# First norm's factor applied to token-major rows on VectorE and the rows transposed on TensorE, with new orders on every engine

## The reference

```python
h = _ln(x, ln1_g, ln1_b)                      # 16 heads of 16, rotary embedding, causal
a = _attn(rope(h @ sa_wq + sa_bq) * scale, rope(h @ sa_wk + sa_bk), h @ sa_wv + sa_bv)
x = x + (a @ sa_wo + sa_bo)
h = _ln(x, ln2_g, ln2_b)                      # queries from h, keys and values from the context y
a = _attn(rope(h @ ca_wq + ca_bq) * scale, rope(y @ ca_wk + ca_bk), y @ ca_wv + ca_bv)
x = x + (a @ ca_wo + ca_bo)
h = _ln(x, ln3_g, ln3_b)
x = x + (gelu(h @ fc1_w + fc1_b) @ fc2_w + fc2_b)
attn = softmax(ctx @ x.T); ti = attn @ x      # scores of the context against the result
out = tanh(cat([ctx, ti]) @ trans_W + trans_b) + ctx
```

## Time and profile before

| what | value |
|---|---|
| median of 3 runs | 3593.34 us (3587.76 to 3603.11) |
| profiled execution | 3593.57 us, its span 3591.8 us |
| granted TensorE clock, mean | 0.907 of 2.4 GHz |
| busy: PE, PEld, DVE, ACT, POOL | 84%, 72%, 63%, 63%, 27% of the span |
| moved by DMA | 173.42 MB, mean 48 GB/s |

### The profile page before, as it was taken

How to read it: one execution, slowest core, us unless ns; L and a number is a source line. 1 busy time by engine, 2 the same in 40 slices (tenths; PEclk the granted TensorE clock), 3 DMA queues, 4 the chain that set the end, 5 groups by cost and what they waited for, 6 DMA issues and landing times.

```text
span 3591.8 us, 92602 instructions
## 1 busy us (share of the span) xinstructions
PE 3031.7 (84%) x38640; PEld 2587.0 (72%) x38640; DVE 2256.0 (63%) x5290; ACT 2271.7 (63%) x4874; POOL 960.5 (27%) x1164
## 2 busy tenths in 40 slices
PE   3578888888888888888888888888888888888897
PEld 3457777777777777777777777777777777777786
DVE  3466666666666666666666666666666666666673
ACT  1246666666666666666666666666666666666676
POOL 1222222222222222222222222222222223223221
PEclk6778989989999999999999999999899899899899
DMA  3111111111111121111111211111111211111110
GB/s 93 36 42 43 47 54 45 47 54 45 47 53 45 47 55 46 50 51 45 50 51 47 53 46 47 53 47 45 53 45 47 53 45 46 53 46 47 52 32 27
DMA packets 299731, 173.42 MB, mean 48 GB/s; under 512 B 68100, under 2 KB 297476, under 8 KB 299044
## 3 DMA queue, kind: packets, MB, share of 16 engines
q1 hardware_dynamic: 298448, 164.36, 16.9%
q10 hardware_dynamic: 864, 3.15, 0.2%
HBM read 81.31 MB, written 16.84 MB: 27 GB/s over the span
## 4 chain that ended last, share of the span: by engine, by line
DMA 39%; PE 25%; DVE 17%; SPq 7%; issue 4%; ACT 4%; POOL 3%; another core or an unknown queue 0%; DVEq 0%; POOLq 0%
DMA rstd_rows<-rstd 22%; DMA rb<-rstd_rows 12%; DVE z_s L740 6%; DMA qkt_s<-rp_s 4%; SPq L242 4%; SPq L249 3%; DVE z_c L740 3%; PE B L384 3%; PE A L610 2%; PE A L384 2%; PE B L386 2%; PE B L385 2%; PE C L384 2%; PE C L385 2%; PE C L386 2%
## 5 line engine op out<-in xcount | busy, mean ns | idle before, releaser
L1061 ACT ACTIVATE pt<-sc 128x512 f32<-128x512 f32 x1024 | 528.9, 603 | 122.2 <-PE sc L413 88.3
L1239 POOL TENSOR_TENSOR rstd<-var_eps,mhalf 128x1 f32<-128x1 f32 x384 | 269.3, 701 | 834.2 <-DVE var_eps L659 834.2
L1234 POOL TENSOR_TENSOR rp_s<-tq_s,cst 128x512 f32<-128x512 f32 x128 | 166.7, 1302 | 837.3 <-ACT tq_s L1053 837.3
L898 DVE TENSOR_TENSOR rows_in<-rows_in,rb 128x256 f32<-128x256 f32 x128 | 57.4, 449 | 420.0 <-DMA rb<-rstd_rows 419.9
L740 DVE TENSOR_REDUCE z_c<-sc 128x8 f32<-128x1024 f32 x256 | 300.7, 1217 | 24.1 <-PE sc L413 24.0
L740 DVE TENSOR_REDUCE z_s<-sc 128x8 f32<-128x1024 f32 x256 | 300.9, 1218 | 0.6 <-PE sc L403 0.6
L1041 ACT CAST qk_bf_s<-qkt_s 128x1024 bf16<-128x1024 f32 x128 | 135.2, 1056 | 245.8 <-DMA qkt_s<-rp_s 245.8
L1041 ACT CAST qk_bf_c<-qkt_c 128x1024 bf16<-128x1024 f32 x128 | 134.8, 1053 | 227.0 <-DMA qkt_c<-rp_c 227.0
L1234 POOL TENSOR_TENSOR rp_c<-tq_c,cst 128x512 f32<-128x512 f32 x128 | 163.4, 1276 | 324.8 <-ACT tq_c L1053 324.8
L413 PE MATMUL sc<-qk_bf_s 31*128 31x128 bf16 x2048 | 59.5, 242 | 216.1 <-ACT qk_bf_s L1041 216.0
L413 PEld LDWEIGHTS sc<-qk_bf_s 31*128 31x128 bf16 x2048 | 34.0, 102 | 264.2 <-ACT qk_bf_s L1041 243.6
(11 more groups left out here) (207 smaller groups left out, 11126.7 us busy)
## 6 DMA issues: line engine op xcount, KB each, us to landing
rows_in<-in_ctx_t SPq DMA_DIRECT2D x256, 128.0 KB, 2.8
qkt_s<-rp_s SPq DMA_DIRECT2D x512, 64.0 KB
qkt_c<-rp_c SPq DMA_DIRECT2D x512, 64.0 KB, 3.6
rows_in<-in_x SPq DMA_DIRECT2D x128, 128.0 KB, 2.9
rows_in<-in_x_t SPq DMA_DIRECT2D x128, 128.0 KB, 2.1
out<-o_out SPq DMA_DIRECT2D x128, 128.0 KB, 3.0
rb<-rstd_rows SPq DMA_DIRECT2D x128, 64.0 KB, 4.8
qkt_s<-zt_s SPq DMA_DIRECT2D x512, 2.0 KB
```

Source lines behind the costliest of these rows:

```text
L1061: act.activation(pt[:, r, :, :].rearrange("p g q -> p (g q)"), sc[:, r, :], ACT.Exp).then_inc(signal, 1)
L1234: pool.tensor_tensor(rp[c][:, :].rearrange("p (a q) -> p a q", q=P), tq[c][:, :].rearrange("p (a q) -> p a q", q=P), rope_c[:, :].unsqueez ...
L1239: pool.tensor_tensor(out[:, :], var_eps[k - 1][:, :], mhalf[:, :], ALU.pow).then_inc(s[f"rs{k}"], 1)
```

## The change

- `x_t`, its load, `rstd_rows`, `rb`, `rbw_`, `rbr_` and `xs_` are gone. `xn_` on DVE multiplies the token-major rows `x_in` by the factor of their partition, `trx1_` on TensorE transposes the result into bank `A0`, and `xt_hi_` and `xt_lo_` read from there.
- `xt_hi` and `xt_lo` hold three tiles; `sq_` takes its pair from them as a view of two thirds, in one pair of three with a backward stride.
- The rings change: `x_in` 5 (3), `ct_f` 3 (4), `ct_g` 2 (1), `cw` 9 (11), `xres_c` 4 (3). `ftan_` writes `o_out` and `fout_` adds in place; `fpre` is gone.
- Every engine has a new order, new offsets of its steps, other waits, and other banks for many results: the transposes, `f1a` and `sq` in `A0`, `pv_s`, `y_c`, `vs`, `cvt`, `fy` in `A1`, `cp`, `pv_c`, `y_s`, `f1b`, `fs`, `trfa` in `B0`. There are 144 slots for 142. The work of each step is otherwise the same.

```diff
-        xt_hi, xt_lo = [sb(f"xt_{p}", [P, KC, M * P], F32R) for p in ("hi", "lo")]
+        xt_hi, xt_lo = [sb(f"xt_{p}", [P, KC, 3 * P], F32R) for p in ("hi", "lo")]
...
-            def rbw_(t):
-                if live(t):
-                    sp.wait_ge(s["rs1"], done(t))
-                    sp.dma_start(rstd_rows[t % 4].unsqueeze(1), rstd1[t % 2][:, :]).then_inc(rbw[t % 2], 16)
-            def rbr_(t):
-                if live(t):
-                    sp.wait_ge(rbw[t % 2], 16 * (t // 2 + 1))
-                    sp.dma_start(rb[t % 2][:, :], rstd_rows[t % 4].partition_broadcast(P)).then_inc(rbr[t % 2], 16)
...
-            def xs_(t):
-                if live(t):
-                    dve.wait_ge(ld_t[t % 2], 16 * (t // 2 + 1))
-                    dve.wait_ge(rbr[t % 2], 16 * (t // 2 + 1))
-                    rows = xt_f[t % 2].rearrange("p (k q) -> p k q", k=KC)
-                    dve.tensor_tensor(rows, rows, rb[t % 2][:, :].unsqueeze(1).broadcast_to([P, KC, P]), ALU.mult).then_inc(s["xs"], 1)
+            def xn_(t):
+                if live(t):
+                    dve.wait_ge(s["rs1"], done(t))
+                    dve.tensor_scalar(xn[:, :], x_in[t % 5], rstd[0][:, 0:1], None, ALU.mult).then_inc(s["xn"], 1)
...
+            def trx1_(t):
+                if live(t):
+                    if t <= 4:
+                        pe.wait_ge(s["xn"], done(t))
+                    if t <= 4:
+                        need(pe, s["tq_s"], pairs(t - 1))
+                    need(pe, s["x2t_lo"], done(t - 5))
+                    transposes(A0, xn[:, :], KC).then_inc(s["trx1"], 1)
...
+            def xt_hi_(t):
+                if live(t):
+                    act.wait_ge(s["trx1"], done(t))
+                    copy(third(xt_hi, t), per_k(A0), s["xt_hi"])
...
+            def pair_of(a, t):
+
+                first = (t - 1) // M * M % 3
+                thirds = [a[:, k, :].rearrange("p (j q) -> p j q", j=3) for k in range(KC)]
+                return [v[:, ::-2, :] if first == 2 else v[:, first:first + M, :] for v in thirds]
...
+                    pair_projection(A0, "sqk", 2 * ((t - 1) % M), pair_of(xt_hi, t), pair_of(xt_lo, t)).then_inc(s["sq"], 1)
```

More of the change, by code:

```diff
@@ L158, in build @@
         zd_s, zd_c = [[sem(f"zd_{c}{i}") for i in range(2)] for c in "sc"]
-        names = ("st1", "mv1", "ve1", "rs1", "xs", "xt_hi", "xt_lo", "vs", "v_s", "sq", "tq_s", "cos_s", "rot_s", "add_s",
+        names = ("st1", "mv1", "ve1", "rs1", "xn", "trx1", "xt_hi", "xt_lo", "vs", "v_s", "sq", "tq_s", "cos_s", "rot_s", "add_s",
                  "kr_s", "p1s", "max_s", "zt_s", "p2s", "exp_s", "pv_s", "ot_s", "rinv_s", "att_s", "norm_s",
@@ L448, in f2, with f2a_ @@
                 mm.then_inc(signal, 1)
[L450 to L464, removed]
             def trx2_(t):
                 if live(t):
-                    if t <= 6:
-                        pe.wait_ge(s["x2n"], done(t))
-                    transposes(A1, x2n[:, :], KC).then_inc(s["trx2"], 1)
+                    pe.wait_ge(s["x2n"], done(t))
+                    transposes(A0, x2n[:, :], KC).then_inc(s["trx2"], 1)
+            def f2a_(t):
+                if live_pair(t):
+                    if t >= TILES - 5:
+                        pe.wait_ge(s["hla"], pairs(t))
+                    f2(t, 0, "a", s["f2a"])
             def p2s_(t):
@@ L519, in p2c_, with trx3_, f2b_ @@
                     heads(qkt["c"][:, t % 4, G:2 * G, :], qkt["c"][:, t % 4, 0:G, :], 2 * HD, True).then_inc(s["p2c"], 1)
+            def trx3_(t):
+                if live(t):
+                    if t >= TILES - 4:
+                        pe.wait_ge(s["xh3"], done(t))
+                    need(pe, s["xt_lo"], done(t + 9))
+                    transposes(A0, xhat[:, :], KC).then_inc(s["trx3"], 1)
+            def f2b_(t):
+                if live_pair(t):
+                    if t >= TILES - 6:
+                        pe.wait_ge(s["hlb"], pairs(t))
+                    f2(t, 1, "b", s["f2b"])
             def y_c_(t):
@@ L580, in p1c_, with trf_ @@
                     pe.wait_ge(s["kr_c"], done(t))
[L581 removed]
+                    if t <= 3:
+                        need(pe, s["max_s"], 2 * done(t + 3))
                     heads(qk_bf["c"][:, 0:G, :], qk_bf["c"][:, G:2 * G, :], MX, True).then_inc(s["p1c"], 1)
[L584 removed]
+            def trf_(t):
                 if live(t):
[L586 to L588 removed]
+                    if t >= TILES - 4:
+                        need(pe, s["x3"], pairs(t + 2) // 2)
+                    need(pe, s["tq_s"], pairs(t + 12))
+                    if t >= TILES - 6:
+                        need(pe, s["ghia"], pairs(t + 3))
+                    transposes(A0, x3[t % R][:, :], KC).then_inc(s["trf"], 1)
@@ L1335, in layouts @@
     out["ctx_t"] = by_feature(out.pop("ctx_1024"))
-    out["x_t"] = by_feature(out["x"])
     def halves_first(w):
```

839 lines of the change are left out of this document (410 added, 429 removed).

## The result

The kernel after takes 2827.38 us (median of 3 runs, 2826.17 to 2829.15) where the kernel before takes 3593.34: a ratio of 0.787, 95% interval 0.784 to 0.789. The direction, the mechanism and the new bound are as forecast; the size is not.

What follows compares the result with a forecast made beforehand. It took the latency of the rstd_rows/rb round trip as the bound, TensorE's queue next: 25 set-up + 224 fill + 114 x 22.1 (2519) + 207 end = 2975 us of span, 2977 us in all; range 2885 to 3230.

Steps and rivals of the forecast that it cites:

- `sq`'s 3-D operand: Operand pairs of sq read on TensorE as a 3-D pattern, one in three with backward stride; cost taken as 0.
- Rival A: New order of ACT or DVE becomes the bound; TensorE idles up to 2.3 us a slot: 24.0, 3210 us; chance 22%.
- B: TensorE was already the bound, the transposes add 40 us: 3633 us, slower; 6% together with dearer 3-D operands.
- C: Another transfer, the four of zt_c before the spread, keeps the period at 26.7: about 3600 us; chance 4%.
- period: Steady time per tile, set by TensorE: 21.39 plus 0.31 for transposes plus 0.37 for hand-overs, 22.07, say 22.1 us.
- fill of 14 slots: First 14 part-filled slots of the pipeline, at 16 us each, the middle between 11.6 and 21.4: 224 us.
- drain: End after the last full slot: 185 us of before plus 22 for one more slot, 207 us.
- the 0.37 us a tile for small hand-overs: TensorE's waits for ot_c and xt_lo in the steady part of before, added to the new slot: 0.37 us a tile.
- the gapless slot: Slot in the old kernel's drain after the last round trip, TensorE busy without a gap: 21.39 us, the period's base.
- `trx1` at 0.31 us: Two added transposes of xn on TensorE, priced like trx2's spacing, nothing hidden: 0.31 us a tile.
- floor, 21.6: Slot behind the range's lower end: 21.6 us with a fill of 200, giving 2885 us.
- ACT's room: ACT's work between f1b's end and p2c's start, about 7.6 us against TensorE's 8.4: fits by 0.8 us.

Runs made afterwards that it cites:

- e1: Kernel before, old orders, without the round trip's write and read; rows of ones replace the factor: 2866.3 us, ratio 0.809.
- e11: Kernel after with x2n and xhat on ACT computing only 32 of their 256 columns: 2827.19 us, ratio 0.820 to before.
- e4: Kernel after with the two transposes of xn (trx1) made twice: 2850.33 us, ratio 0.805 to before.
- e8: Kernel after without trx1 and xn; x_t loaded again, factors turned on DVE, sent through DRAM in four pieces: 2822.92 us, ratio 0.817 to before.
- e5: Kernel after with x2n computed twice on ACT in each slot: 2888.66 us.
- e10: Kernel before, old orders, factors turned on DVE and written as four pieces of 128 bytes, read as before: 2950.45 us, ratio 0.854.
- e9: Kernel before with the 128 factors written 64 bytes apart; the read takes an input row instead: 2884.74 us.
- e7: Kernel after with the old round trip put back at the end of SP's slot, xn waiting for it: 4064.99 us.
- e2: Kernel before with both transfers still issued, but DVE doesn't wait for them and multiplies by ones: 3396.9 us.
- e3: Kernel before with the 128 factors written 512 bytes apart; the read takes an input row instead: 2883.63 us.

## Why the prediction was off

What held: the mechanism (the round trip bounded the kernel, TensorE's queue comes next) and its signs, namely no `rstd_rows` and no `rb` in the chain; the chain 94% TensorE; clock 0.99 over the span; no wait of `kr_s` for its spread (it lands in 2.2 us, not the 3.6 taken); nothing lost by `sq`'s 3-D operand: its group takes 1.61 us in every pair of the kernel after, and as much in e1 where it isn't held up. Rival A fell by the period and by e11, B by e1, C by the period.

The profiled execution took 2829.15 us for its span of 2827.4, the same 1.8 outside it that the prediction added. So the miss is taken between the spans, 2975 - 2827 = 148 us, and it goes by terms:

| term | predicted | measured | us in the total |
|---|---|---|---|
| period | 22.1 | 21.093 | 113 x 1.007 = 114 |
| full slots | 114 | 113 | 22 |
| set-up | 25 | 21.1 | 4 |
| fill of 14 slots | 224 | 222.6 | 1 |
| drain | 207 | 200.1 | 7 |

The period is the term that failed, and in three parts of it. First, the 0.37 us a tile for small hand-overs, carried over from the steady part of before: in e1 none of them shows as a wait of the matmuls, and what is left of `xt_lo`'s is within its 21.33. It was within the 21.39 of the drain too (there `xt_lo` ends at 3416.69 and `sq` starts at 3416.74). So the gapless slot was the right base as it stood, and to add hand-overs to it was the mistake. Second, `trx1` at 0.31 us: 0.207 by e4, 0.15 by e8. Third, a part that the prediction put at nothing: the new order itself. The kernel after less `trx1` has 21.093 - 0.207 = 20.89, the old order in e1 21.33, with the same matmuls and a granted clock of 1.00 in both. That is 0.44 us a tile, 50 us in all; by e8, which has no `trx1` and 20.97, it is 0.36. With 0.06 of the base (21.39 for 21.33) and 0.03 of rounding (22.07 to 22.1) the parts make up the 1.007. In a slot of each, `trx2` takes 0.31 of the queue in e1 and 0.14 in the kernel after, `trf` 0.31 to 0.37 and 0.19, `trx3` 0.27 to 0.37 and 0.19, `y_s` and `y_c` 0.96 and 0.86; `cp`, `f2a` and `fs` are 0.08 to 0.17 dearer. So what a group costs depends on what stands beside it. 0.13 of the 0.44 is the hidden wait of `sq` for `xt_lo` in the old order. Whether the rest is a cost of the change of form from one group to the next, or further waits under modelled ends, no run tells apart: e11 excludes `x2n` and `xhat` as a source of it in the new order, and the old order wasn't tried with less on ACT or DVE. This part of the cause stays open.

The second line of the table is a miscount. The prediction's own paragraph on the ends counts 113 periods from the 15th `xs` to the last; its sum has 114, and 22 us for the slot more in the drain besides.

The range failed by the same step. Its floor, 21.6, can only be the old slot plus a cheap `trx1`: it took the old order's slot as the least that the same matmuls can need. A floor that gave a new order of the same matmuls half a microsecond in either direction (21.1, 57 us less in all) and counted 113 slots (22 less) would have stood at 2806 and held the time.

Two things held only by luck. One is ACT's room: the walk gave 0.8 us and measured are about 0.1; it ended at `exp_s` and passed over the hand-over of `x2n`, which came earlier. With 0.6 us more on ACT the time would have been 2889 (e5). The other is the fill: 16 us a slot was the middle between two bounds and not worked out, and the old order without its trip (e1) took 246.5 us for the same stretch, not 224.

Three readings were wrong and did not move the forecast. The period of before is 26.84 and not 26.67, so the account of the steady slot doesn't close but leaves about 0.2 us over. With it, the 15th `xs` starts at 369.0 us and not at 393, and the fill of before took 24 us a slot and not 26. And the earlier trace rows show the write of tile 1, not of tile 0, whose write took from 12.05 to 26.00 among the loads of the weights; that tile 1's is as slow with little in flight still holds.

## What to carry to other kernels

When a wait is removed and a stretch of the trace shows the kernel without it and without a gap, take that stretch's slot as it stands; waits of the disturbed part are a consequence, or are in it already, and aren't added again, and a new order of the same matmuls gets a margin to both sides. Read the waits of the weight loads beside those of the matmuls: a slot with TensorE busy throughout can still hold waits. Before a transfer is designed away, look at what its pieces share: here turning the 4-byte pieces into four rows recovers 80% of the gain with a few lines (e10), and spacing them by 64 bytes makes the write as short (e9), though a kernel that reads them back from there wasn't run. And to price a transfer, walk the loop that it closes, with everything queued before it on its issuer (e7) and everything queued beside it (e2), not its own latency.

## What the runs showed of the hardware

A write of 128 separate factors of 4 bytes took 8.07 us with the factors side by side and 1.5 us with 64 or with 512 bytes between their starts (e3, e9); one 64-KB transfer issued beside the slow write took 8.1 us, and the median is 2.2 once it is gone (e2, e3). The read back of the same 512 bytes took 4.8 us (median) behind the slow write and 3.1 behind one of four pieces (before, e10); why isn't shown. Two 128x128 f32 transposes cost 0.15 to 0.21 us of TensorE's time in a stream (e8, e4), and the granted clock stayed at 1.00 with eleven of them a tile (e4). The same matmuls in another order took 0.36 to 0.44 us of 21.3 less, with no gap to be seen in either. A wait of 0.34 us for `xt_lo` on every second tile showed as idle time of the weight loads (0.39 us) and not of the matmuls (e1). And the kernel that hangs on the latency of its transfers differed by 4% between the five groups of runs (3447 to 3593 us), the one bound by TensorE by 0.1% (2827 and 2830); four of the five groups ran on different chips, and the chip of the first isn't recorded.
